# A decoder layer on one core: GpSimd computes the scan's inflow two tiles ahead instead of one

## The reference, cut to what matters

```python
def step(h, inp):
    d_t, b_t, c_t, u_t = inp
    h = h * jnp.exp(d_t[:, :, None] * A) + (d_t * u_t)[:, :, None] * b_t[:, None, :]
    y = jnp.einsum('bdn,bn->bd', h, c_t)
    return (h, y)
```

## Time and profile before

| | us |
|---|---|
| median of 3 runs | 1484.77 (1480.97 to 1487.95) |
| profiled execution, time | 1483.81 |
| profiled execution, span | 1482.1 |
| VectorE busy in the span | 933.1 (63%) |
| TensorE busy | 1031.7 (70%) |
| GpSimd busy | 771.7 (52%) |
| ScalarE busy | 632.3 (43%) |
| mean granted TensorE clock | 0.844 |

### The profile page before, as it was taken

One profiled execution on the slowest core, in us unless ns is written; L12 is line 12 of the kernel. 1 busy time (PEld: TensorE's weight loads), 2 busy tenths in 40 slices (PEclk: granted clock), 3 DMA queues, 4 the chain that ended last, 5 costly groups with the idle time before them and its releaser, 6 DMA issues. The chain is left out here.

```text
span 1482.1 us, 19685 instructions
## 1 busy us (share of the span) xinstructions
PE 1031.7 (70%) x4626; PEld 827.7 (56%) x4626; DVE 933.1 (63%) x1524; ACT 632.3 (43%) x1532; POOL 771.7 (52%) x684
## 2 busy tenths in 40 slices
PE   4567769778679678678677767206777777787556
PEld 2445548567567567567566555105666666665344
DVE  1798987988888888888888813323333333333246
ACT  3574655745635636546544221102333443343200
POOL 0444554556656657647758573333555555555400
PEclk8698889989889789889879886557999999889878
DMA  6634635430230220321221011117766675765387
GB/s 225 211 111 144 185 121 161 142 100 32 70 111 32 91 91 34 103 75 50 91 72 49 34 54 51 38 59 240 208 214 190 202 214 174 225 207 178 101 308 259
DMA packets 118415, 194.91 MB, mean 132 GB/s; under 512 B 17685, under 2 KB 83379, under 8 KB 115923
## 3 DMA queue, kind: packets, MB, share of 16 engines
q1 hardware_dynamic: 79890, 134.54, 29.1%
q0 software_dynamic: 16512, 35.19, 6.5%
q10 hardware_dynamic: 21952, 24.51, 5.3%
HBM read 155.21 MB, written 75.64 MB: 156 GB/s over the span
## 5 line engine op out<-in xcount | busy, mean ns | idle before, releaser
L406 POOL TENSOR_TENSOR inf<-bc,du 128x1024 f32<-128x1024 f32 x128 | 304.6, 2379 | 216.4 <-DVEq L1000 168.1
L763 PE MATMUL Y<-hb,ident 128*128 128x256 f32 x1024 | 282.7, 427 | 65.2 <-DVE u L1018 40.9
L1002 DVE TENSOR_TENSOR_SCAN DA<-DA,inf 128x1024 f32<-128x1024 f32 x128 | 293.4, 2292 | 52.6 <-POOL inf L406 38.2
L1386 POOL DMA_INDIRECT yp_dram<-ys,pid x216 | 210.1, 973 | 207.4 <-ACT ys L1459 101.9
L763 PEld LDWEIGHTS Y<-hb,ident 128*128 128x128 f32 x1024 | 218.2, 217 | 113.2 <-DVE hb L1009 29.6
L590 ACT ACTIVATE DA<-dl,a_neg 128x255 f32<-128x255 f32 x512 | 211.7, 460 | 0.2
L1426 PE MATMUL DA<-wt,h 128*128 128x256 f32 x432 | 146.8, 425 | 53.3 <-ACT h L1452 42.8
L1419 PE MATMUL DA<-xgT,wt 128*128 128x128 f32 x864 | 152.4, 304 | 42.0 <-DVE xgT L1561 25.1
L462 POOL DMA_INDIRECT xe_dram<-x2e,ad_i x128 | 130.8, 1022 | 62.8 <-issue 34.9
L1009 DVE TENSOR_TENSOR hb<-DA,bc 128x1024 f32<-128x1024 f32 x128 | 156.4, 1222 | 10.4 <-DVE DA L1002 0.5
L1419 PEld LDWEIGHTS DA<-xgT,wt 128*128 128x128 f32 x864 | 126.0, 210 | 57.0 <-DVE xgT L1561 30.5
(11 more groups left out here) (258 smaller groups left out, 1556.3 us busy)
## 6 DMA issues: line engine op xcount, KB each, us to landing
wt<-in_w_moe SPq DMA_DIRECT2D x216, 256.0 KB
bc<-bc_dram SPq DMA_DIRECT2D x32, 1024.0 KB, 5.4
xg_all<-xe_dram SPq DMA_DIRECT2D x216, 140.0 KB
Y<-yp_dram SPq DMA_DIRECT2D x16, 1024.0 KB, 6.1
xe_dram<-zeros ACTq DMA_DIRECT2D x2, 7420.0 KB, 24.7
xe_dram<-zeros ACTq DMA_DIRECT2D x1, 7560.0 KB, 25.3
yp_dram<-ys,pid POOLq DMA_INDIRECT x216
xt<-in_xT SPq DMA_DIRECT2D x8, 256.0 KB, 3.8
```

Of the source, the lines that this page charges most:

```text
L406: g.tensor_tensor(inf[t % NI][:, :, :], bc[gr][:, 0, :, :], du[p][:, c, :].unsqueeze(1).to_broadcast([P, SG, T]), ALU.mult).then_inc(inflo ...
L763: ins = mm(Y[:, 0:T], ident[:, :], hb[t % NH][:, n, :], start=gr == 0 and n == 0, stop=gr == NG - 1 and n == SG - 1, skip_group_check=True)
L1002: v.tensor_tensor_scan(da[:, :], da[:, :], inf[t % NI][:, :, :].rearrange("p n t -> p (n t)"), 0.0, ALU.mult, ALU.add).then_inc(scan_d.sem, 1)
L1386: g.indirect_dma_start(yp_dram, bass.IndirectOffsetOnAxis(ap=pid[:, half * UNROLL + s_:half * UNROLL + s_ + 1], axis=0), ys[s_][:, :], Non ...
```

## The change

The number of tiles by which GpSimd runs ahead is 2 instead of 1, and the inflow of tile t waits for the gate of one scan earlier: for t-1 releases instead of t. There are 4 inflow buffers before and after.

```diff
-LEAD_I = 1
+LEAD_I = 2
...
-                if scan_go.at(b, t, True):
-                    pool.wait_ge(scan_go.sem, scan_go.at(b, t))
+                if scan_go.at(b, t - 1, True):
+                    pool.wait_ge(scan_go.sem, scan_go.at(b, t - 1))
                     pool.sem_inc(tick, 1)
```

## The result

The changed kernel took 1464.81 us (median of 4, 1457.72 to 1468.78) against 1483.97 of the kernel before (4 runs): ratio 0.9864, 95% interval 0.9818 to 0.9910. Two repeats on other chips gave 0.9854 (0.9834 to 0.9875) and 0.9891 (0.9857 to 0.9925). The profiled execution took 1466.17 against 1483.81, so 17.6 us less; forecast were 10.8.

The account below looks back on a forecast made before the run. VectorE was taken as the bound, with 38.2 us of waits before scans as upper limit. Gains 0.6 (turn 1) + 6.4 (turn 3) + 0 (turns 4 to 6) + 3.8 (turn 7) = 10.8 us, so 1474.0; range 1460 to 1482, the forecast's own 1470 to 1477.

Parts of the forecast that it names:

- Slot 11 gives nothing: Slot 11, turns 3 to 6: VectorE waits for the norm instead, its addition still ends at 499.57 (turn 4); gain 0.
- Slot 5, turns 4 and 6: Scan 5 starts earlier, but an inflow holds off the conv's fourth operation; conv about 4.4 instead of 1.98, gain 0.
- Slot 5, turn 5: Treated like slot 5 of turn 4: conv held off by GpSimd's inflow, gain 0.
- I take it as blocked: Slot 5, turn 4: fourth conv operation held off by the inflow at 459.54, its distance 0.54 against 0.53 in nearest rows.
- the rival: Conv slips through in turns 4 to 6 too: 22.5 us gained, 1462.3; one such turn 1470; chance 0.25.
- the row: Turn 4, before slot 7's inflow (469.14): second conv operation ended 468.61, third started 468.54 and ran until about 473.0.
- The rival's price for such a turn: If slot 5's conv slips through, 3.9 us stays per turn, TensorE limiting, with two operations of slot 6's conv caught.
- Turn 3: Slot 5's longer wait, 4.78, lets both convs clear the inflows: 9.7 us gained at scan 7, 6.4 kept.
- Turn 7: No conv: 1.5 us before slot 9's root, 1.35 at tile 14's inflow, 0.9 at the gate operation; sum 3.8.
- Turns 0 to 2: Gain 0.6 in turn 1, 0 in turn 2; earlier requests for the next batch's tiles at slots 14, 15 cost 0.
- rival "slower": Late bc at slots 14 and 15 delays GpSimd; about 1493 with 3 us in five turns and no gain; chance 0.04.
- GpSimd's instructions keep their order and, where GpSimd was waiting for the gate, their times: All slots: the gate is reached in the same place of VectorE's list; 128 inflows of the same length, nothing added or removed.

Follow-up runs that it names:

- Experiment 3: Changed kernel with the two scatters of slot 9 issued in slot 10, behind the second norm's multiplication and addition; 1430.68 us, ratio to the kernel before 0.9709.
- Experiment 2: Changed kernel with one scatter moved from slot 5 to 4 and one from slot 6 to 5; 1450.72 us, ratio to the kernel before 0.9836.
- experiment 10: Against the changed kernel, the lead of two tiles kept but the old gate (t releases) restored; 1429.16 us, ratio to the kernel before 0.9696.

## Why the prediction was right or wrong

**Slot 11 gives nothing: right.** 4.93 before, 4.94 after, in the parts that the prediction named, though the addition showed 2.81 where I had said 1.75: it now issues at once when the norm ends and is recorded from there. Experiment 3 shows that the GpSimd chain was the cause, by removing its parts: 4 to 5 us a turn.

**Slot 5, turns 4 and 6: right, with its mechanism.** Forecast: first conv 4.4, gain 0. Measured: 4.49 and 4.47, and 0.2 and 0.4. Experiment 2, which moves only scatters, had 7 to 8 us a turn back at scan 7 and kept 4.

**Slot 5, turn 5: wrong, and this is the step that failed.** "I take it as blocked" was read off turn 4 at a margin of 0.01 us and then applied to turn 5, where the wait was 0.11 longer and GpSimd stood 0.65 behind instead of 0.54. There the conv passes: 6.2 us, most of the 6.8 by which the profiled difference exceeds the forecast. I had named it as the likeliest turn for the rival, and should have priced the turns one by one. The margin itself was misread too: I set a recorded end in the row (468.61, 0.53 ahead of its inflow) against a third operation that I let end at 459.0, when the fourth starts. A conv operation is recorded 0.47 long at a pace of 0.40, so it would have ended at 459.08. Measured alike, the distances are 0.46 in turn 4, 0.47 in turn 6 and 0.58 in turn 5 against 0.53 in the row: turns 4 and 6 lay on the blocked side of it and turn 5 on the other, which is what happened. The rival's price for such a turn, 3.9 with TensorE as the limit and two operations of the second conv caught, was wrong as well: 6.2 with none caught, 5.2 in each repeat with one. By recorded starts VectorE was first in turn 4 as well (453.20 against 453.81) and lost. The rule of the Trainium skill (SBUF — State Buffer, section Who interferes with whom) that whoever issues first holds the other off agrees with these traces only if the moment of the claim is meant, and not the recorded start.

**Turn 3: right in its parts**, 9.7 at scan 7 as forecast and 6.2 for 6.4 in the end. **Turn 7: right in its parts**, 1.5 at scan 12, 2.9 at scan 14, 3.8 at scan 15, of it the gate operation at 818.07 with 1.50 instead of 2.35. **Turns 0 to 2:** +1.0 instead of -0.6. All of it lies ahead of the first scan (49.8 before, 50.8 after, 48.1 to 51.3 over all runs); the three turns together are as long as before (263.6), though singly they are not steady: turn 1 took 91.5 before, 93.9, 93.4 and 93.5 with the whole change, and 89.3 in experiment 3. A gain of 0.6 can't be told there, and the cause of the spread is open.

**The rest**, 1.8 us behind the last scan in the profiled pair, is within what single executions of one kernel differ there (644.9, 634.8 and 634.0 for the whole change on different chips); no cause was tested.

**Sum:** 10.8 + 6.2 (turn 5) - 1.6 (turns 0 to 2) + 0.6 (turns 4 and 6) - 0.2 (turn 3) + 1.8 = 17.6, the profiled difference.

**The rival "slower"** names about 1493 for 3 us in each of five turns; on 1483.8 these would make about 1499. Nothing of it was seen, and the forecast does not use it.

**What the prediction did not see.** I costed the change as one piece and found its two halves harmless to each other. They are not: the lead removes the waits, the weaker gate lets GpSimd start inflows ahead of VectorE's two-input operations and costs 29 us (1458.06 against 1429.16; 41 us of longer operations, less 14 of idle, in the windows of experiment 10). That "GpSimd's instructions keep their order and, where GpSimd was waiting for the gate, their times" was true against the kernel before; it hid that a lead of two with the old gate would have put them in a better place.

## What to carry to other kernels

When a stall goes, follow the freed engine to the next operation that the other engine can hold off; here that turned 3.6 us of idle in slot 5 of turn 4 into 3.7 us of longer conv (2.5 and 1.2), and when the conv was freed, 3.6 us came back in an operation on two columns. Busy time does not show it: compare an operation's length with its shortest elsewhere. A gate between two such engines also decides which of them is held off: running further ahead and loosening the gate are separate decisions, to be timed separately. A margin under 0.1 us in a replay has to be taken for each turn by itself, and the distances compared have to be measured alike, end with end or start with start: here turn 5 differed from 4 and 6 every time, and one place of it fell either way.

## What the runs showed of the hardware that was not expected

An inflow queued behind an indirect transfer holds off VectorE's conv operations before its own recorded start: caught were those whose predecessor ended 0.45 us or more after the transfer's recorded start, passed those at 0.41 and 0.32, and the inflow's own start is about 1.0 behind the transfer's. It is the inflow that does it: in experiment 2's turn 4 the third operation is 0.05 ahead of a scatter (455.21, 455.26), as close as where the fourth was caught, but another scatter follows instead of an inflow, and the fourth takes 0.47. An inflow that waits for a gate held nothing off before its start in the one place read: in the kernel before, with an inflow from 235.56, a conv operation that had started 0.05 earlier passed, and the inflow took 2.64 instead of 2.36. Where one side gives way can be read off: either the conv operation shows 3 to 4.5 us, or the indirect transfer shows 1.15 to 1.25 instead of 0.96. And not only operations with two SBUF inputs are held off: the TENSOR_SCALAR on 128x2 values, with one, took 3.97 instead of 0.17.
